# Attention and expert layer on one core: the products of probabilities and values issued in pairs of head groups

## What is computed

```python
q = (layernorm(x) @ Wq.T + bq).reshape(B, S, H, Dh).transpose(0, 2, 1, 3)
A = einsum('bhqd,bhkd->bhqk', q, k) / sqrt(Dh)        # masked above the diagonal
w = softmax(A, axis=-1)
x = x + einsum('bhqk,bhkd->bhqd', w, v)... @ Wo.T + bo
gate = softmax(layernorm(x) @ router_w.T), top 4 kept
x = x + shared experts + gated routed experts
```

## Time and profile before

| | |
|---|---|
| median of 3 runs | 226.51 us (225.4 to 226.7) |
| the profiled execution, its own time | 225.0 us |
| its span | 223.0 us |
| TensorE busy | 188.8 us, 85% |
| VectorE busy | 169.8 us, 76% |
| ScalarE busy | 143.2 us, 64% |
| GpSimd busy | 96.2 us, 43% |
| chain that ended last, by engine | PE 49%, DVE 16%, SP queue 9%, issue 8%, ACT 7%, POOL 5%, DMA 5% |
| mean granted TensorE clock | 0.985 |

### The profile page before, as it was taken

The page is one execution under the profiler, slowest core; times in us unless marked ns, Lnnn a source line. Parts: engine busy times, 40 slices in busy tenths (PEclk is TensorE's granted clock), DMA queues, the critical chain, the costliest instruction groups (busy, mean ns, idle before and its releaser), DMA issues.

```text
span 223.0 us, 4896 instructions
## 1 busy us (share of the span) xinstructions
PE 188.8 (85%) x1610; PEld 138.3 (62%) x1610; DVE 169.8 (76%) x456; ACT 143.2 (64%) x276; POOL 96.2 (43%) x178
## 2 busy tenths in 40 slices
PE   0629788869999978978999999886969989999992
PEld 0316565557777746756676776455848858787871
DVE  4599978619689859959989996227968688787781
ACT  2261365726586885875777768875867976777661
POOL 5789029906457577577566565732202000000000
PEclk9999999958999999999999999999999999999999
DMA  4523333830332311312312210100000010010011
GB/s 128 155 70 99 82 95 84 259 101 19 97 84 55 105 44 50 103 47 50 99 54 75 78 31 3 31 6 24 3 1 0 3 50 0 0 47 0 0 48 47
DMA packets 23735, 12.97 MB, mean 58 GB/s; under 512 B 4696, under 2 KB 23400, under 8 KB 23712
## 3 DMA queue, kind: packets, MB, share of 16 engines
q1 hardware_dynamic: 23040, 12.52, 20.4%
q10 hardware_dynamic: 576, 0.13, 0.3%
q0 software_dynamic: 96, 0.03, 0.1%
HBM read 3.86 MB, written 1.05 MB: 22 GB/s over the span
## 4 chain that ended last, share of the span: by engine, by line
PE 49%; DVE 16%; SPq 9%; issue 8%; ACT 7%; POOL 5%; DMA 5%; POOLq 0%; DVEq 0%; ACTq 0%
SPq L328 6%; DVE sb_mx L765 5%; PE psum L955 5%; PE psum L937 3%; PE psum L874 3%; PE psum L871 3%; PE psum L914 3%; PE psum L872 3%; PE psum L856 3%; PE psum L858 3%; PE psum L857 3%; DMA sb_ctx<-in_ctx_t 2%; PE psum L863 2%; PE psum L921 2%; PE psum L918 2%
## 5 line engine op out<-in xcount | busy, mean ns | idle before, releaser
L765 DVE TENSOR_REDUCE sb_mx<-psum 128x2 f32<-128x512 f32 (+1 forms) x96 | 62.8, 678 | 10.3 <-PE psum L921 8.1
L577 ACT ACTIVATE sb_probs<-psum 128x512 f32<-128x512 f32 x96 | 55.8, 602 | 20.7 <-PE psum L937 19.0
L422 POOL TENSOR_SCALAR_AFFINE_SELECT sb_probs<-sb_probs 128x256 f32<-128x256 f32 (+1 forms) x96 | 45.2, 487 | 36.5 <-ACT sb_probs L577 35.8
L656 DVE TENSOR_TENSOR sb_probs<-sb_probs,psum 128x512 f32<-128x512 f32 x32 | 21.9, 683 | 10.1 <-ACT sb_probs L521 9.8
L521 ACT ACTIVATE sb_probs<-psum 128x512 f32<-128x512 f32 x36 | 21.5, 600 | 12.0 <-PE psum L858 11.9
L914 PE MATMUL psum<-sb_qk_op 96*128 96x256 bf16 x128 | 26.0, 286 | 0.0
L937 PE MATMUL psum<-sb_qk_op 128*128 128x256 bf16 x128 | 24.8, 276 | 0.9 <-ACT sb_probs L577 0.7
L663 DVE TENSOR_TENSOR sb_hid_l<-sb_probs,sb_hid_h 128x512 fp32r<-128x512 f32 x36 | 24.7, 685 | 0.3
L527 ACT CAST sb_hid_h<-sb_probs 128x512 fp32r<-128x512 f32 x36 | 22.2, 616 | 2.9 <-DVE sb_probs L656 2.9
L911 PE MATMUL psum<-sb_fut,sb_id_b 128*128 128x256 bf16 x64 | 18.4, 287 | 5.3 <-issue 4.4
L955 PE MATMUL psum<-sb_probs,sb_v_op 128*32 128x256 f32 x256 | 20.5, 391 | 0.8 <-ACT sb_o_raw L552 0.8
(11 more groups left out here) (114 smaller groups left out, 390.0 us busy)
## 6 DMA issues: line engine op xcount, KB each, us to landing
sb_qk_op<-sb_qk SPq DMA_DIRECT2D x96, 64.0 KB
sb_ctx<-in_ctx_t SPq DMA_DIRECT2D x8, 128.0 KB, 2.4
sb_num<-sb_o_raw SPq DMA_DIRECT2D x8, 128.0 KB, 2.1
out<-sb_o_raw SPq DMA_DIRECT2D x4, 256.0 KB, 2.3
sb_x<-in_x SPq DMA_DIRECT2D x3, 256.0 KB, 4.2
sb_up_f<-in_rup_t SPq DMA_DIRECT2D x1, 512.0 KB, 3.6
sb_dn_f<-in_rdown SPq DMA_DIRECT2D x1, 512.0 KB, 4.4
sb_x<-in_x SPq DMA_DIRECT2D x2, 128.0 KB, 3.4
```

The source lines that it names most:

```text
L422: nc.gpsimd.affine_select(out=v, in_=v, compare_op=ALU.is_ge, fill=0.0, base=0, pattern=[[0, v.shape[1]], [1, P]], channel_multiplier=-1). ...
L577: nc.scalar.activation(probs[g][:, u * BANK:(u + 1) * BANK], psum[:, BANK_S + n % SB, :], ACT.Exp, scale=float(DH) ** -0.5).then_inc(s_exp, 1)
L656: nc.vector.tensor_tensor(hid[buf[k]], gel[buf[k]], psum[:, 3 + k % 2, :], ALU.mult)\
L765: nc.vector.tensor_reduce(dst, src, AX, ALU.max).then_inc(m_max, 1)
```

## The change

The products of two groups are issued directly one after the other. In the ordinary turns groups 0 and 1 of batch at-2 both stand at unit 8 (group 0 stood at unit 5). Groups 2 and 3 both stand at unit 2 of the turn after (they stood at unit 11 of the same turn and unit 1 of the next), and read 1 moves from unit 1 to unit 2. In turn 9 the pairs stand at units 2, 4 and 7 in place of units 1, 3, 4, 6, 7. The call now takes the side from the parity of the batch, which is the same value as before. The number and the form of the instructions stay.

```diff
             if last_scores(turn):
-                steps = {1: [(c3, 3)], 3: [(c2, 0)], 4: [(c2, 1)], 6: [(c2, 2)], 7: [(c2, 3)]}
+                steps = {2: [(c3, 2), (c3, 3)], 4: [(c2, 0), (c2, 1)], 7: [(c2, 2), (c2, 3)]}
             elif isinstance(turn.at, int) and turn.at > NB + 1:
                 steps = {}
             else:
-                steps = {1: [(c3, 3)], 5: [(c2, 0)], 8: [(c2, 1)], 11: [(c2, 2)]}
+                steps = {2: [(c3, 2), (c3, 3)], 8: [(c2, 0), (c2, 1)]}
...
             if last_scores(turn):
-                steps = {1: [(c3, 1)], 5: [(c2, 0)], 8: [(c2, 1)]}
+                steps = {2: [(c3, 1)], 5: [(c2, 0)], 8: [(c2, 1)]}
...
-                steps = {1: [(c3, 1)], 9: [(c2, 0)]}
+                steps = {2: [(c3, 1)], 9: [(c2, 0)]}
...
-                        pv(c, turn.side(3 if g == 3 and not (last_scores(turn) and t > 1) else 2), g)
+                        pv(c, c % 2, g)
```

## The result

The changed kernel took 227.18 us (median of 18 runs, 224.56 to 228.42) against 225.33 us for the kernel before (18 runs, 223.51 to 226.7) in the same series. The ratio is 1.0069, 95% interval [1.0036, 1.0102]: slower, by less than the 1% bound, so "same" by the classes of the prediction, which had 0.27 for it against 0.63 for slower. 227.18 lies inside the range of 226.5 to 232.5; the forecast of 230.3 was 3.1 us too high, and the change of 1.85 us is half of the 3.8 that was forecast.

A forecast was written before the change was run, and what follows sets the result against it. Turns were taken as bound by several nearly full engines and an equally long loop through SP. Accumulated shifts of +1.7, +2.7, +2.1, +2.9, +3.1 and +3.8 us, the last added to the 226.51 median, gave 230.3; range 226.5 to 232.5.

The forecast's parts named there:

- Part 1: Adjacent product groups on TensorE: fewer tile-shape changes save 0.3 us for the unit 8 pair where TensorE ends the turn.
- Part 2: Turn 3: pair behind the context wait runs at half clock, denominators leave late; +2.0 us at unit 7, +1.7 at end.
- the bounds: Uncertain costs: turn 3 costs 0.7 us at full clock, not 2.0; total from about +0.2 to about +6.
- Part 3: Denominators-to-operands loop through SP: 15.25 us against 14.75; accumulated shift +2.7 at turn 4's end, +2.9 in turn 7.
- Part 4: Turn 8: pair at unit 2 delays the denominators; accumulated +3.4 us at unit 7, +3.1 at the end; the turn itself +0.2.
- Part 5: Turn 9: ScalarE idles 0.9 us at unit 2 and 0.65 at unit 4, less other gaps removed; net +0.7 us.
- The first, that the denominators come in time: Rival at L791: VectorE arrives as late as the DMA in turns 4, 7, 8; +1.2 us, 227.7; chance 0.22.
- The gain of shape changes: Rival on TensorE: two pairs a turn save 0.3 us each in turns 3 to 9; 222.3 us, chance 0.10.
- ran dry: Rival at unit 8: the pair holds back VectorE's maxima, 0.5 us in six turns, 3.0 more; 233.3 us, chance 0.13.

The follow-up runs named there:

- x12: Kernel before with group 0 moved to unit 8 and group 1 to unit 9, not adjacent; 230.16 us, ratio 1.020.
- x2: Kernel before with only the pair of groups 0 and 1 at unit 8; 227.93 us, ratio 1.0123.
- x15: Kernel before with groups 0 and 1 paired at unit 7, ahead of L967, all else unchanged; 223.65 us, ratio 0.9918.
- x7: Kernel before with only groups 2 and 3 paired at unit 2, turn 9 with its old places; 227.02 us, ratio 1.0075.
- x1: Changed kernel with turn 9's old places, the extra group 2 of batch 6 put in front of group 3; 228.14 us, ratio 1.0127.
- x9: Changed kernel with group 2 of batch 6 left at unit 11 of turn 8; 227.20 us, ratio 1.0054.
- x14: Kernel before with the pairs in turn 9 alone, without the extra group; 225.33 us, ratio 1.0018.
- c_after: The repeat: the unmodified changed kernel timed and profiled a second time, against the kernel before; 227.82 us, ratio 1.0102.
- x8: Changed kernel with batch 0's groups 2 and 3 and their copy back at their old places around turn 3; 226.43 us, ratio 1.0028.
- x3: Changed kernel with the second pair at unit 1, ahead of the project, also in turn 9; 226.18 us, ratio 1.0037.

## Why the prediction was right or wrong

| step | forecast | measured (changed - before) |
|---|---|---|
| turn 3 | +1.7 | +1.27, repeat +0.20; +2.06 and +0.82 from the arrival of the context |
| turn 4 | +1.0 | -0.05 |
| turns 5, 6 | -0.3 each | +0.06, +0.06 (repeat 1.65, with the stretch at the lower clock, and +0.06) |
| turn 7 | +0.8 | -0.18 |
| turn 8 | +0.2 | +1.04, repeat +0.49 |
| turn 9 | +0.7 | +0.83, repeat +0.84 |
| time | +3.8 | +3.1 in the profiled executions, +1.85 in the medians |

**The level.** Of the 3.1 us by which 230.3 was too high, 1.2 has nothing to do with the change. I added the 3.8 to a median of three runs, 226.51; the median of 18 runs of the same kernel is 225.33, near the profiled 225.0. The first sum, 228.8, would have been 1.6 too high. The other 1.95 us are the change itself: 3.8 forecast, 1.85 measured. That 227.18 fell inside the range is owed to its width, not to the parts.

**Part 1 (fewer changes of tile shape): size right, value wrong.** Adjacent groups start 0.64 to 0.68 us apart, and x12 against x2 gives 0.34 us in three turns where I took 0.3. What failed is the step that let this be the only effect of unit 8: "putting two together saves ... I take 0.3 for the pair at unit 8 wherever TensorE sets the end of the turn". I priced the shape change and not the place. Group 0 had stood in the shadow of L967's wait; out of it, the pair costs 0.5 to 0.6 us a turn net (x2), and one unit earlier, in the shadow, it gains 0.15 to 0.5 in turns 4 to 8 (x15). The rows to see it were in the trace: L967 at unit 7 waited 0.17 us *with* group 0 ahead of it.

**Part 2 (turn 3): mechanism right, size right only from the arrival of the context.** In the first profile both groups run at the level of 1.2 GHz, 2.7 us together (2.56 + 0.25 forecast), L791 waits, L967 has 1.19 us of idle ahead of it, and from the arrival of the context it is 2.06 where 2.0 at unit 7 and 1.7 at the end were forecast. Two things make the turn's loss smaller. "The load lands when it did" did not hold: the context came 0.79 us earlier, so +1.27 is left. And not every execution has the low clock at the pair: in the repeat it takes 1.44 us, and from the context it is +0.82, near the 0.7 that the bounds gave for the full clock.

**Part 3 (the loop through SP): wrong; it does not exist.** I took the 0.45 us ahead of L568 as a wait for the operand transfers of the batch before, as that row names a DMA. The changed kernel refutes it: ScalarE's L568 runs while SP is still issuing them.

```profile
64.14 0.47 ACT L568 ACTIVATE sb_qk<-psum,sb_bq 128x256 bf16<-128x256 f32 x1 [0.27 <-DMA sb_qk_op<-sb_qk]
```

```profile
61.04 3.99 SPq L328 DMA_DIRECT2D sb_qk_op<-sb_qk  x6
```

The wait in the code is for the transfers two batches back, long done (for batch c it asks for `96 * (c - 1)`, and each batch adds 96 per half), and so the description ahead of the prediction, which says the batch before, is wrong too. What ends last is TensorE's project: before, L981 starts at 111.78 and takes 0.59, to 112.37, and L568 starts at 112.42. In x15 the same wait carries the right name:

```profile
111.04 0.48 ACT L568 ACTIVATE sb_qk<-psum,sb_bq 128x256 bf16<-128x256 f32 x1 [0.44 <-PE psum L981]
```

Without the loop nothing had to repeat every 15.25 us, and L379 to L379 in the changed kernel is 14.63 (54.68 to 69.31) and 14.97 us (103.00 to 117.97). VectorE does wait for the denominators, as forecast, in turns 3, 4, 7 and 8, but 0.8 us each time (up to 3 was forecast for turn 3), and turns 4 and 7 did not get longer by it:

```profile
117.58 0.35 DVE L791 RECIPROCAL sb_rden<-sb_den 128x32 f32<-128x32 f32 x1 [0.78 <-DMA sb_den<-sb_o_raw]
```

In the kernel before VectorE had a wait of nearly the same size shortly ahead of it in both turns, for scores behind the project, and it is gone now that no group stands ahead of the project:

```profile
64.30 0.69 DVE L765 TENSOR_REDUCE sb_mx<-psum 128x4 f32<-128x512 f32 x1 [0.60 <-PE psum L921]
...
112.86 0.69 DVE L765 TENSOR_REDUCE sb_mx<-psum 128x4 f32<-128x512 f32 x1 [0.61 <-PE psum L921]
```

So one wait took the place of another; that this is why the turns kept their length is my reading, and no run shows it by itself. This part carried +1.8 us of the forecast in turns 4 and 7, less the 0.6 that turns 5 and 6 were to return; measured were -0.05 and -0.18, and +0.12 for turns 5 and 6. It is the main error.

**Part 4 (turn 8): too small, for another reason.** The late denominators are there: L791 starts 6.28 us behind the L802 of turn 7 (5.30 before). Each half of the change lengthens turn 8 by itself, x2 by 0.50 with the pair at unit 8 and x7 by 0.76 with the pair at unit 2, and there are the operand transfers that SP begins later. TensorE's wait for them was 1.08, 0.61, 0.46, 0.16 and 0 us in the profiles of the changed kernel, x2, x1, x9 and the repeat, with the transfers issued at the same point of the turn to within 0.1 us in the first, in x9 and in the repeat: when they land varies by up to 1 us between executions. How much of the 0.5 to 1.0 us is either pair, the denominators or these transfers is not settled.

**Part 5 (turn 9): number right, mechanism half wrong.** 0.7 forecast, 0.83 measured. ScalarE idles 0.86 and 0.71 us in the changed kernel, close to the 0.9 and 0.65 of the forecast:

```profile
144.04 0.59 ACT L552 COPY sb_o_raw<-psum 128x512 f32<-128x512 f32 x1 [0.86 <-PE psum L958]
...
147.86 1.09 ACT L577 ACTIVATE sb_probs<-psum 128x512 f32<-128x512 f32 x2 [0.71 <-PE psum L937]
```

But with the pairs and without the extra group turn 9 costs 0.16 (x14), and with the group and without the pairs 0.67 (x1). So the 0.9 at unit 2 stands for the group that turn 9 takes over and does not hand on, which I had not named, and the 0.65 at unit 4, the mark of the pairs, costs 0.16 at most. That the sum came out is partly luck.

**The rivals.** The first, that the denominators come in time and only turns 3 and 9 stay (+1.2), is nearest to the +1.85 of the medians, though not for its reason: they come late, and it costs little in turns 4 and 7. The gain of shape changes exists (x15), only not at these units. VectorE hardly ran dry behind the pair at unit 8: it waits 1.12 us for scores in turn 3 (0.76 before) and 0.35 in turn 8, and not in turns 4 to 7.

## What to carry to other kernels

Before moving work on a full engine, find the wait that its old place was covering: a small wait right behind it can mean that the place is nearly free, and here a saving of 0.3 us at another place did not pay for it. Test a loop through queues against the code's own counts and against the end times of each candidate, since the name of a releaser is inferred. When turns hand work to each other, count what the first and the last give and take.

## What the hardware showed that I had not expected

The granted clock is not a function of the kernel alone. The second profile of the changed kernel has a stretch at the lower level in turn 5 and the first has none, although TensorE's waits in that turn are the same: 0.47 us at L911 and 0.98 or 0.99 at L967 in both. The two executions differ before that, in turn 3: from 48 to 52 us the granted clock is 0.52 in the first profile and 0.90 in c_after. First the windows of c_after (turn 5), then those of the first profile:

```profile
75.40:84.00 8.60, 7.25 (x84) 5.36 (x82) 5.43 (x16) 7.78 (x16) 6.01 (x8) 1.00 0.25 69
84.00:88.00 4.00, 2.83 (x21) 1.99 (x21) 3.90 (x15) 1.74 (x4) 3.40 (x7) 0.80 0.13 30
88.00:92.00 4.00, 4.00 (x47) 2.74 (x47) 2.43 (x10) 1.52 (x3) 0.90 (x2) 0.78 0.28 75
```

```profile
76.40:85.00 8.60, 7.31 (x84) 5.41 (x82) 5.45 (x16) 7.82 (x16) 5.95 (x8) 1.00 0.25 70
85.00:89.00 4.00, 2.79 (x37) 2.00 (x41) 3.90 (x15) 1.77 (x5) 3.43 (x7) 1.00 0.13 29
89.00:93.40 4.40, 4.25 (x55) 3.33 (x47) 4.27 (x14) 2.94 (x6) 1.92 (x5) 1.00 0.36 98
```

The stretch cost 1.57 us (18.61 against 17.04 in turn 6 of the same execution, where before had 16.96 and 16.98). Like stretches appear in some executions of most kernels here, in turn 3, in turn 5 or in the last 70 us. Four of twelve executions of x8 and five of twelve of x3 had a mean clock of 0.998 or more, and none of 23 executions of the kernel before in either series. So a change can move the median by how often such stretches occur, and a difference of under 1.5 us between two single executions of this kernel says little unless their mean clocks agree. Even then it is not safe: at 0.984 and 0.985 the spans of the kernel before go from 222.8 to 224.7 us.
